# A learned tensor-product layer of a graph network: units innermost, feature-major scans, repacked weight pieces, and chunk work placed between tiles

## What is computed

```python
# x: 8 scalars + 8 vectors of 3 per node; edges are sorted by edge_dst
xs = concat([x[edge_src, :8], x[edge_dst, :8]])                    # 16 scalars (units)
xv = concat([x[edge_src, 8:].reshape(E, 8, 3), x[edge_dst, 8:]...])  # 16 vectors
y1, y2 = _sph(edge_vec)              # from the unit vector n of the edge
h = sqrt(2) * relu(emb @ W1 / sqrt(10))                            # 16 hidden units
w = (h @ W2 / 4).reshape(E, 7, 16, 8)                              # 7 weight sets per edge
s_out = PW_S * (xs.wa_s + (xv.y1).wb_s / sqrt(3))                  # 8 per edge
g_out = PW_S * (xs.wa_g + (xv.y1).wb_g / sqrt(3))                  # 8 gates
v_out = PW_V * (xs y1 .wc / sqrt(3) + xv.wd / sqrt(3) + (xv y2 W3J).we)   # 8 x 3
ftr = concat([1.593 tanh(s_out), 1.593 tanh(g_out) * v_out]) * norm
out = segment_sum(ftr, edge_dst)
```

## Time and profile before

| what | us |
|---|---|
| median of 3 runs | 17684.24 (17683.38 to 17685.33) |
| profiled execution | 17735.37 |
| its span | 17733.5 |
| third layer in it: first transposes to last product | 11504.85 to 16663.95 |

### The profile page before, as it was taken

How to read it: one execution, slowest core, us unless ns; L and a number is a source line. 1 busy time by engine, 2 the same in 40 slices (tenths; PEclk the granted TensorE clock), 3 DMA queues, 4 the chain that set the end, 5 groups by cost and what they waited for, 6 DMA issues and landing times. The chain is left out here.

```text
span 17733.5 us, 130262 instructions
## 1 busy us (share of the span) xinstructions
PE 8686.6 (49%) x48544; PEld 5340.9 (30%) x48544; DVE 6077.6 (34%) x9968; ACT 1162.1 (7%) x2044; POOL 7510.9 (42%) x7030
## 2 busy tenths in 40 slices
PE   2333330000089899999300000066676776666699
PEld 2333320000044444444200000044444454444444
DVE  4666660000000001010133333256565565655600
ACT  0000000000000000000000000011111111111100
POOL 5787777777710100001477777623323223232210
PEclk6555555555599998999555555578787887888799
DMA  4444440000077776777211111101011011010077
GB/s 147 165 165 165 165 140 2 0 0 0 4 263 276 258 280 243 266 269 267 55 35 33 33 37 30 26 11 22 17 22 18 16 22 18 16 23 17 30 266 258
DMA packets 709944, 1808.29 MB, mean 102 GB/s; under 512 B 419038, under 2 KB 497108, under 8 KB 601012
## 3 DMA queue, kind: packets, MB, share of 16 engines
q1 hardware_dynamic: 468292, 1571.06, 25.7%
q0 software_dynamic: 224288, 153.60, 4.7%
q10 hardware_dynamic: 16848, 76.28, 1.1%
HBM read 1423.24 MB, written 377.52 MB: 102 GB/s over the span
## 5 line engine op out<-in xcount | busy, mean ns | idle before, releaser
L180 POOL DMA_INDIRECT z_l<-table,idx_l x1568 | 1548.1, 987 | 3450.4 <-DMA z_l<-start_rows 2963.6
L1653 PE MATMUL p_r<-prod,ident 128*128 128x128 f32 x12544 | 1820.4, 289 | 1114.5 <-issue 852.6
L180 POOL DMA_INDIRECT g_l<-table_l,idx_l x1568 | 1966.8, 1254 | 524.9 <-issue 504.7
L1800 DVE TENSOR_TENSOR prod<-p_t,h_l 128x768 f32<-128x768 f32 x1568 | 1435.5, 951 | 2101.3 <-remote 1283.6
L1653 PEld LDWEIGHTS p_r<-prod,ident 128*128 128x128 f32 x12544 | 1708.1, 203 | 1236.4 <-issue 1166.8
L180 POOL DMA_INDIRECT g_gat<-table,idx_gat x1568 | 1694.5, 1081 | 653.7 <-issue 527.9
L788 POOL DMA_INDIRECT adj<-worth,sq x1568 | 1543.9, 985 | 566.5 <-issue 510.6
L918 PE MATMUL p_h<-w_s,emb_s 10*128 10x16 f32 x3136 | 678.4, 369 | 1375.4 <-ACT hid L944 1083.2
L1643 PE MATMUL p_t<-wv,zvt 112*128 112x384 bf16 x4704 | 1110.3, 345 | 132.5 <-issue 132.2
L1340 PE MATMUL pr<-diag,ones 128*128 128x256 f32 x2 | 1.2, 714 | 2391.4 <-DVE diag L1358 2391.4
L346 PE MATMUL pc_l<-spread,cross_lo 128*128 128x448 f32 x28 | 25.3, 1022 | 2248.9 <-DVE spread L350 2084.7
(11 more groups left out here) (427 smaller groups left out, 10285.7 us busy)
## 6 DMA issues: line engine op xcount, KB each, us to landing
adj<-zeros SPq DMA_DIRECT2D x28, 8232.0 KB
cells_cheb0a<-adj SPq DMA_DIRECT2D x168, 1344.0 KB
cells_cheb0b<-adj SPq DMA_DIRECT2D x168, 1344.0 KB
cells_cheb1a<-adj SPq DMA_DIRECT2D x168, 1344.0 KB
cells_cheb1b<-adj SPq DMA_DIRECT2D x168, 1344.0 KB
cells_l<-adj SPq DMA_DIRECT2D x168, 1344.0 KB
gat_rows<-prod_gat ACTq DMA_DIRECT2D x28, 952.0 KB
start_rows<-zeros SPq DMA_DIRECT2D x28, 896.0 KB
```

The source lines that it names most:

```text
L180: return pool.indirect_dma_start(out=dest, out_offset=None, in_=table_ap, in_offset=bass.IndirectOffsetOnAxis(ap=index, axis=0))
L1653: last = nc.tensor.matmul(p_r[:], ident[:], prod[q % 2][:, 2:6, :, k, :].rearrange("p g t w -> p (g t) w"), start=(k == 0), stop=(k == 15))
L1800: V.tensor_tensor(prod[q % 2][:, :, t], p_t[tile % 3][:, :, 0:3 * KM], h, ALU.mult).then_inc(t_used, 1)
```

## The change

- **Layouts.** `prod` is (group, tile, w, k) with the 16 hidden units innermost. The weights are set up with columns in that order. DVE's reduction now reads 16 neighbours; the sums of PE read `prod[:, 2:6, :, :, k]`, one float32 out of every 16.
- **Packed pieces.** The scalars fill rows 0 to 111 and the vectors rows 0 to 127 of their transposed tiles, with further copies of the high parts, so that a tile is products of 384, 384, 384, 128 and 384 columns, all with 128 rows. ACT copies one [128, 1024] tile per quad instead of two of [.., 512].
- **The chunk's start.** The first quad of the next chunk is turned inside the last quad of this one (after t=1), with the wait on `z_split` there. `low` moves from q=13 to q=10 and 11.
- **Scans.** The table of nodes, the start rows and the directions are written component-major by the layers before. Rows are turned to (feature, edge) by ACT, and 16 features are scanned by one instruction of 896 elements against a mask that is zero at each feature's first edge; a small instruction adds the carried value. Fill and messages are two scans each per chunk, instead of 32.
- **Placing.** What DVE does per chunk stands in single instructions after t=1 or t=3 of a tile; the reduction of quad q-1 stands after the first tile of quad q. ACT does its chunk work in half-quad steps and issues the store of the messages from its own queue; the message result is turned back by ACT.
- **Around it.** `gat_norm_stage` makes the component-major copy of each of its 7 blocks with two copies on DVE.

```diff
-                prod = [sb(f"prod{b}", [P, NG, 4, 16, M]) for b in range(2)]
+                prod = [sb(f"prod{b}", [P, NG, 4, M, 16]) for b in range(2)]
...
-                            for half, lhs, parts in ((0, zst[q % 2], ((ws[0], NS), (ws[1], 64))),
-                                                     (1, zvt[q % 2], tuple((w, NV) for w in wv))):
-                                for k, (w, rows) in enumerate(parts):
-                                    last = nc.tensor.matmul(p_t[tile % 3][:, half, 0:3 * KM], lhs[0:rows, col], w[0:rows, :],
-                                                            start=(k == 0), stop=(k == len(parts) - 1))
+                            nc.tensor.matmul(into[:, 0, 0:3 * KM], lhs_s, ws[0][:], start=True, stop=False)
+                            nc.tensor.matmul(into[:, 0, 0:3 * KM], lhs_s, ws[1][:], start=False, stop=True)
+                            nc.tensor.matmul(into[:, 1, 0:3 * KM], lhs_v, wv[0][:], start=True, stop=False)
+                            nc.tensor.matmul(into[:, 1, 2 * KM:3 * KM], lhs_s, wx[:], start=False, stop=False)
+                            nc.tensor.matmul(into[:, 1, 0:3 * KM], lhs_v, wv[1][:], start=False, stop=True).then_inc(t_made, 1)
...
-                                                        prod[q % 2][:, 2:6, :, k, :].rearrange("p g t w -> p (g t) w"),
+                                                        prod[q % 2][:, 2:6, :, :, k].rearrange("p g t w -> p (g t w)"),
...
-                            pe.wait_ge(z_split, c + 1)
-                            transposes(c, b, 0)
...
-                                    if t == 1 and q + 1 < Q:
-                                        transposes(c, b, q + 1)
+                                    if t == 1:
+                                        if q + 1 < Q:
+                                            transposes(c, b, q + 1)
+                                        elif more:
+                                            pe.wait_ge(z_split, c + 2)
+                                            transposes(c + 1, 1 - b, 0)
...
-                            A.activation(zst[q % 2][:], p_z[:, 0, :], ACT.Copy)
-                            A.activation(zvt[q % 2][:], p_z[0:NV, 1, :], ACT.Copy).then_inc(zt_ready, 1)
+                            A.activation(zt[q % 2], p_z[:], ACT.Copy).then_inc(zt_ready, 1)
...
-                            return V.tensor_reduce(th[b][:, :, 4 * q:4 * q + 4, :],
-                                                   prod[q % 2][:, 0:2].rearrange("p g t k w -> p g t w k"), AX.X, ALU.add)
+                            last = V.tensor_reduce(out6[b][:, 0:2, :, 4 * q:4 * q + 4].rearrange("p g w t -> p g t w"),
+                                                   prod[q % 2][:, 0:2], AX.X, ALU.add)
...
-                            for f in range(*THIRDS[part]):
-                                last = V.tensor_tensor_scan(msg[:, :, f], same[:, bass.ds(c * CH, CH)], msg[:, :, f],
-                                                            tail[:, f:f + 1], ALU.mult, ALU.add)
+                                V.scalar_tensor_tensor(msgf[:, :, 0], tail[:, 0:D], same0[:, 1:2], msgf[:, :, 0], ALU.mult, ALU.add).then_inc(s_msg, 1)
+                                v.wait_ge(s_msg, c * MSG + 6)
+                                V.tensor_tensor_scan(flat_msg[0], flat_mask[0], flat_msg[0], 0.0, ALU.mult, ALU.add)
```

More of the change, by code:

```diff
@@ new lines, in fill_mask_half, with msg_mask_half @@
+                        def fill_mask_half(c, half, first=False):
+                            if half == 0 and not first:
+                                act.wait_ge(msg_done, c - 2)
+                            made = mask_half(c, half, 0)
+                            if half == 1:
+                                made.then_inc(fill_mask, 1)
+                        def msg_mask_half(c, half):
+                            made = mask_half(c, half, 1)
+                            if half == 1:
+                                made.then_inc(msg_mask, 1)
@@ L1736, in _ @@
                         act.sem_inc(zt_ready, 1)
                         act.sem_inc(red_out, 1)
-                        high(0, 0)
-                        low(0, 0)
+                        for half in range(2):
+                            fill_mask_half(0, half, first=True)
+                        for half in range(2):
+                            starts_half(0, half)
+                        for half in range(2):
+                            dst_half(0, half)
+                        for step in range(6):
+                            high(0, 0, step)
@@ L1740, in _ @@
+                        for step in range(3):
+                            low(0, 0, step)
+                        turn(0, 0, first=True)
                         one_chunk(0, 0, first=True)
-                        with act.Fori(0, n - 1) as i:
+                        one_chunk(1, 1, second=True)
+                        with act.Fori(1, n - 1) as i:
+                            one_chunk(2 * i, 0)
                             one_chunk(2 * i + 1, 1)
-                            one_chunk(2 * i + 2, 0)
+                        one_chunk(2 * n - 2, 0)
@@ L1874, in _ @@
+                        v.sem_inc(fill_done, 1)
+                        for half in range(2):
+                            fill_scan(0, half)
+                        for e in range(2):
+                            p_terms(0, 0, e, 0, first=True)
+                        for step in range(2):
+                            p_sum(0, step)
+                        for step in range(3):
+                            leave(0, 0, step)
                         one_chunk(0, 0, 0, before=False)
-                        with v.Fori(0, n - 1) as i:
+                        one_chunk(1, 1, 1, second=True)
@@ L1876, in _ @@
+                        with v.Fori(1, n - 1) as i:
+                            one_chunk(2 * i, 0, i)
                             one_chunk(2 * i + 1, 1, i + 1)
-                            one_chunk(2 * i + 2, 0, i + 1)
+                        one_chunk(2 * n - 2, 0, n - 1)
                         one_chunk(2 * n - 1, 1, n, more=False)
-                        messages(2 * n - 1, 1, last=True)
-                        for part in range(3):
-                            message_sums(2 * n - 1, part)
@@ L1882, in l2_pass @@
-            close(s_v, 1 + 2 * n * TAIL)
-            for b in range(2):
-                close(loaded[b], 32 * n)
-                close(stored[b], 16 * n)
+                        reduced(2 * n - 1, 1, Q - 1)
+                        for step in range(6):
+                            message(2 * n - 1, 1, step)
         with ExitStack() as st:
```

596 lines of the change are left out of this document (374 added, 222 removed).

## The result

The changed kernel takes 18292.78 us (median of 4 runs) against 17683.81, a ratio of 1.0345 with a 95% interval of 1.0325 to 1.0366: slower by 3.4%. The forecast was 17,170. One of the four runs took 19,769 us at a lower granted clock (0.623 against 0.724), and the ratio leaves it out. The profiled execution took 18,298 us, 562 more than that of before, and all of the difference is there when the third layer ends: its last sum ends at 17,230 instead of 16,668.

What follows compares the result with a forecast made beforehand. PE was taken to bound a clean chunk (130.9 us, becoming 111.3), with 55.5 us of gather loss kept. 26 chunks give -510, last -11, first -5, once-only costs +15: -511, so 17,170 us; 8-in-10 range 16,930 to 18,700.

Steps and rivals of the forecast that it cites:

- rival 1: PE's sums slow down reading `prod` floats 64 bytes apart: 39 to 59 us a chunk, about 18,560 us; chance 0.37.
- Products: PE's products per tile, 1664 columns instead of 1920: saving 0.11 to 0.30 us a tile, taken as 0.16.
- The extra 0.19 us of the scalar pair: PE's two scalar products take 0.19 us more than their 768 columns at the vector pace; it may stay.
- The chunk's start and the message block: PE's waits of 6.1 us for ACT's last low copy and 3.1 us behind DVE's message block both go.
- VectorE: DVE's reduction takes 1.16 us and each scan 2.2; DVE falls to about 90 us of a chunk, no bound.
- The backlog: DVE lags PE by 3.2 us over quads 5 to 7; charged 4 us a chunk, bounds 0 to 9.
- ScalarE: ACT's turning and masks bring it to some 40 us a chunk; PE's waits charged 2 us, bounds 0 to 5.
- The chunk without a price for the sums' read: A clean chunk, with the strided read free, takes 105.3 + 4 + 2 = 111.3 us, 19.6 less.
- The gather loss: Time a chunk loses while POOL gathers, PE, DVE and ACT nearly stopping: left at 55.5 us.
- rival 2: Gather loss changes: +15 us a chunk, 17,560 us (chance 0.05), or 10 us shorter, 16,910 (0.02).
- the main case: The forecast itself, strided read free: 17,170 us, within this case 16,900 to 17,450; chance 0.51.
- Rival 3: DVE's dealt-out work holds PE up, each of 14 extras costing 1.3 us: about 17,660 us; chance 0.05.

Runs made afterwards that it cites:

- r2: Changed kernel with `prod` laid out so that PE's sums read runs of 2 float32 instead of lone ones; 15366.67 us, 0.9657 of the kernel before in its set.
- r8: Changed kernel with `prod` laid out as before the change, PE's sums reading runs of 8 float32; 15532.08 us, 0.9763 of the kernel before in its set.

## Why the prediction was wrong

**The step that failed** is the choice in the sum to take the sums' strided read as free, at 0.51 against 0.37. The mechanism of rival 1 was what happened. Its price was right in size: 39 to 59 us a chunk, taken as 50; measured 448 records x 104 ns = 47. Its threshold, 163 ns a record, was passed with 216. I had one row for it (L1804: 1.96 ns an element in steps of 32 bytes) and one against it (L1822: 9% more for an operand in long steps). I let the second count as much as the first, though L1822 reads w after w of three rows in turn, and may find lines again that it has just read; nothing tests that here. L1804 was the nearer row: one stream, one float32 per line, in the same tile. Its factor over neighbours was 1.7, and PE's is 1.9.

**By the other steps:**

- *Products*: 0.16 us a tile forecast, within 0.11 to 0.30; measured 0.30, the good end. The extra 0.19 us of the scalar pair is gone; whether it was the 64-row form or the mix of 112 and 128 rows wasn't separated.
- *The chunk's start and the message block*: both waits went, as forecast. Undone in `r2`, they cost some 3 to 6 and 2 us a chunk. What the old code lost at both went with other parts too: the shorter reduction, the low copies in steps.
- *VectorE*: reduction 1.21 us (forecast 1.16), scans 2.02 (2.2), busy 93 us in a clean chunk (90). The scan's 2.25 ns an element are about twice the 1.16 of L1823. The backlog, charged at 4 us, doesn't show in the changed kernel, where PE is slow enough. In `r2` PE waits 6 us for DVE in chunk 26.
- *ScalarE*: busy 45.7 us (forecast 40), and no wait of PE for it in the clean chunk.
- *The chunk without a price for the sums' read*: forecast 111.3, which is 19.6 less. `r2` is that case, with quick sums and a quick reduction: 107.9 against 128.0 for the old chunk in sets without the loss, 20.1 less, and 542 us less in all, where 511 were forecast. That the two agree so well is in part luck: the products alone are 8 us a chunk better than forecast, so other terms are some 4 worse, which no run takes apart, and the old chunk is 3 us shorter there. `r8`, whose reduction is slow as before, has 114.0, and 377 us less in all. So the rest of the sum was sound in size, and the strided read alone turned its sign.
- *The gather loss*: left at 55.5 us; it is 207.0 - 145.8 = 61, so rival 2 went a third of its way. Its picture, handshakes that take tens of microseconds, is what the trace shows in the stall: counts of PE that arrive 23 to 59 us late.
- *The whole*: 24 x (207.0 - 186.4) = +494; chunk 0, into which 152 gathers fall now, 327.6 instead of 246.7, +81; chunk 25, with no gathers left to hold it up, -39; chunks 26 and 27 +36; the first transposes 18 us earlier. Together 554 of the 562. Rival 1's 18,560 was too high by the products (8 us a chunk) and by the 6 us of waits it took over from the main case.

Rival 3 didn't occur: in chunk 26 of the changed kernel PE hardly waits for DVE, and with the quick sums of `r2` it waits 6 us.

## What to carry to other kernels

When a layout is changed so that one engine reads neighbours, look at every other reader of the tile, and how many float32 of each 16 bytes it takes: two neighbours were free on PE and DVE, a lone one cost 1.9 and 1.65 times. A tile with two readers along different axes can often serve both with pairs innermost. And where GpSimd issues many small gathers in a row beside a long instruction stream, look whether other engines' signals come late meanwhile, and spread the gathers over the work: in a set with the loss it brought the loss from 63 to 17 us a chunk, more than any other part, and in the others it cost nothing. Few packets of instructions in a stall don't show that fetching is the cause: here they came once per 132 instructions of PE, whether it had stood still between or not.

## What was not expected of the hardware

- Reading one lone float32 in every 64 bytes sets PE's pace at 216 to 218 ns for 128 columns, 1.7 ns a column, where a run of 2, 4 or 8 gives 112 ns.
- With gathers in a row, in two of six sets of runs, PE's counts of finished work reach the engines that wait for them up to 59 us late, though the DMA engines are 9% busy; PE, DVE and ACT then stand still for most of 55 us a chunk. In the other sets the same count is never late. The same kernel takes 17,690 and 15,910 us in the two kinds of set.
- Four gathers at a time, released by PE's progress, bring that loss from 63 to 17 us a chunk.
